# Mixture-of-experts kernel: small remainder tiles two to a tile in the last round but one, five token blocks needed before the first tiles, three blocks placed without pauses

## What is computed

```python
x = x + jnp.tanh(g_xattn[0]) * _L0_xattn_ref(ctx_512, _layernorm(x, axis=-1), L0_xattn_W, L0_xattn_b)
x = x + jnp.tanh(g_ffn[0]) * _L0_ffn_ref(_layernorm(x, axis=-1), L0_ffn_w_router, ...)

scores = jax.nn.sigmoid(xf @ w_router)
sfc = scores + corr_bias          # choice: 4 best of 8 groups, then the 6 best experts in them
combine = jnp.zeros((T, E), dtype=x.dtype).at[jnp.arange(T)[:, None], topk_idx].add(topk_w)
g = jnp.einsum('th,ehm->etm', xf, gate_w)
u = jnp.einsum('th,ehm->etm', xf, up_w)
eo = jnp.einsum('etm,emh->eth', jax.nn.silu(g) * u, down_w)
routed = jnp.einsum('te,eth->th', combine, eo)
shared = jax.nn.silu(xf @ sh_gate_w) * (xf @ sh_up_w) @ sh_down_w
```

## Time and profile before

| | |
|---|---|
| median of 3 runs | 258.53 us |
| the profiled execution | 258.77 us |
| its span in the profile | 256.9 us |
| TensorE matmuls busy | 219.3 us (85%) |
| GpSimd busy | 157.4 us (61%) |
| VectorE busy | 129.4 us (50%) |
| ScalarE busy | 80.0 us (31%) |
| mean granted TensorE clock | 0.924 |
| gate and up instructions (line 742) | 224, four for each of 56 tiles |
| moved by DMA | 53.72 MB |

### The profile page before, as it was taken

How to read it: one execution, slowest core, us unless ns; L and a number is a source line. 1 busy time by engine, 2 the same in 40 slices (tenths; PEclk the granted TensorE clock), 3 DMA queues, 4 the chain that set the end, 5 groups by cost and what they waited for, 6 DMA issues and landing times.

```text
span 256.9 us, 5093 instructions
## 1 busy us (share of the span) xinstructions
PE 219.3 (85%) x1043; PEld 170.9 (67%) x1044; DVE 129.4 (50%) x528; ACT 80.0 (31%) x222; POOL 157.4 (61%) x188
## 2 busy tenths in 40 slices
PE   7996987994799789999999999999999998996000
PEld 6895776882677467877777777778777776774000
DVE  2898886929554444434443444434343443343334
ACT  3636121011010124343434344344444433442000
POOL 6352888787878873528468488566575665475300
PEclk9779799997599999999999999999999999999555
DMA  6999999999997649999998768777667675257767
GB/s 200 250 260 278 407 376 331 332 373 292 318 351 255 195 151 337 253 303 214 249 231 158 126 112 154 121 121 119 107 117 108 110 119 81 35 64 153 175 168 260
DMA packets 41018, 53.72 MB, mean 209 GB/s; under 512 B 5134, under 2 KB 35438, under 8 KB 40998
## 3 DMA queue, kind: packets, MB, share of 16 engines
q1 hardware_dynamic: 25520, 30.99, 41.7%
q0 software_dynamic: 11280, 18.36, 35.7%
q10 hardware_dynamic: 4198, 4.15, 5.9%
HBM read 31.72 MB, written 21.77 MB: 208 GB/s over the span
## 4 chain that ended last, share of the span: by engine, by line
PE 61%; DVE 17%; DMA 8%; issue 5%; another core or an unknown queue 4%; POOL 4%; ACT 1%; SPq 0%; ACTq 0%; POOLq 0%; DVEq 0%
PE pG L742 26%; PE pY L756 18%; PE pX L736 5%; DMA sum_dram<-xnT,idx 5%; PE pH L750 5%; PE pG L765 3%; PE pY L692 2%; PE pY L784 2%; DMA wgu<-sum_dram 2%; POOL rows_dram L432 1%; DMA wij<-in_L_xattn_W_dram 1%; PE pH L773 1%; DVE wgu L1013 1%; POOL rstd L418 1%
## 5 line engine op out<-in xcount | busy, mean ns | idle before, releaser
L445 POOL DMA_INDIRECT sum_dram<-xnT,idx x56 | 86.7, 1548 | 57.2 <-ACT xnT L559 30.8
L742 PE MATMUL pG<-wgu,sdown 128*128 x224 | 75.8, 461 | 1.4 <-issue 1.4
L432 POOL DMA_INDIRECT rows_dram<-rows,row_i x48 | 47.5, 989 | 18.3 <-issue 11.3
L756 PE MATMUL pY<-wd,sup 88*128 x224 | 57.5, 379 | 0.0
L1134 DVE COPY sup<-pH 88x256 f32<-88x256 f32 x56 | 23.5, 420 | 59.0 <-PE pH L750 51.3
L742 PEld LDWEIGHTS pG<-wgu,sdown 128*128 128x128 f32 x224 | 38.5, 191 | 13.9 <-issue 2.0
L559 ACT ACTIVATE xnT<-pY,wt 128x256 f32<-128x256 f32 x56 | 26.5, 473 | 54.1 <-issue 22.4
L756 PEld LDWEIGHTS pY<-wd,sup 88*128 88x128 f32 x224 | 38.0, 190 | 3.2 <-issue 0.2
L750 PEld LDWEIGHTS pH<-ident,sgate 128*88 128x88 f32 x112 | 18.0, 161 | 13.6 <-DVE sgate L1130 0.5
L552 ACT ACTIVATE sgate<-pG 128x176 f32<-128x176 f32 x56 | 17.8, 317 | 27.1 <-PE pG L742 26.0
L547 ACT ACTIVATE sdown<-pX 128x256 f32<-128x256 f32 x56 | 21.0, 377 | 4.9 <-PE pX L736 4.5
(11 more groups left out here) (183 smaller groups left out, 246.2 us busy)
## 6 DMA issues: line engine op xcount, KB each, us to landing
wgu<-in_L_ffn_gate_w_dram SPq DMA_DIRECT2D x8, 704.0 KB, 10.0
wgu<-in_L_ffn_up_w_dram SPq DMA_DIRECT2D x8, 704.0 KB, 13.0
wd<-in_L_ffn_down_w_dram SPq DMA_DIRECT2D x8, 640.0 KB
sum_dram<-zeros POOLq DMA_DIRECT2D x3, 1152.0 KB
wgu<-sum_dram SPq DMA_DIRECT2D x12, 256.0 KB, 3.9
xg<-rows_dram SPq DMA_DIRECT2D x16, 144.5 KB
rows<-rows_dram ACTq DMA_DIRECT2D x16, 144.5 KB
rows_dram<-zeros SPq DMA_DIRECT2D x8, 289.0 KB, 4.5
```

What stands on the lines that cost most here:

```text
L432: pool.indirect_dma_start(rows_dram[:, :], bass.IndirectOffsetOnAxis(ap=row_i[:, j, k:k + 1], axis=0), lines[:, j * ROW:j * ROW + LINE], N ...
L445: pool.indirect_dma_start(sums_dram[into[s]][:, :], bass.IndirectOffsetOnAxis(ap=idx[:, s:s + 1], axis=0), y[s], None, compute_op=ALU.add) ...
L742: ins = nc.tensor.matmul(pG[par][:, 0:2 * M].rearrange("t (g m) -> t g m", g=2), xT[:, par, k, :], wgu[:, bass.ds(e, 1), :, k, :].rearrang ...
L756: ins = nc.tensor.matmul(pY[par][:, 0:H], hT[0:MI, par, i, :], wd[:, bass.ds(e, 1), i, :], start=(i == 0), stop=(i == I - 1))
```

## The change

**Shared tiles.** The plan has four segments. A remainder of more than 64 rows is still a tile of its own; remainders of up to 64 rows (SIDE = 64) go two to a tile, into the 8 tiles of the round before the last, which has 16 such sides (entries 112 to 127 of the plan's table). Sides beyond 16 would become whole tiles. In such a turn SyncE loads the two halves of the tile apart (`load_sides`), TensorE does gate and up and down for each half in its own half of the array's columns (`gate_up_sides`, `down_sides`, `tile_position=(0, SIDE)`), ScalarE scales the halves apart (`scale_y_sides`), VectorE picks apart (`take_sides`), and GpSimd makes two adds of 64 rows (`add_side`). The first half's expert has its weights in SBUF at an index read from the table; the second half's weights are loaded again from DRAM into a ring of three (gate and up) and a ring of two (down) buffers (`own_gate_up`, `own_down`). The last round holds whole tiles (`load_final`, `take_final`, `add_final`).

**Blocks.** The tiles that may start early are now those for which the first FIRST = 5 blocks suffice, and the first loads wait for five blocks' scatters. The three blocks after them are scattered without the pause.

The core of the diff:

```diff
-    LEAST = -(-(PAIRS - T) // (P * ROUND)) - 1
+    SIDE = P // 2
+    SHARED = P - 2 * ROUND
+    LEAST = HELD + 1
-    REST = 16 * (J - JH) * TOPK
+    FIRST = JH + 1
+    REST = 16 * (J - FIRST) * TOPK
-    SEGS = 3
+    SEGS = 4
     INTO = [s % SUMS for s in range(ROUND)]
-    INTO_LAST = [2, 0, 1, 2, 0, 1, 0, 1]
+    INTO_SIDES = [(q + 2) % SUMS for q in range(2 * ROUND)]
+    INTO_LAST = [0, 2, 1, 2, 0, 1, 0, 1]
...
             last = load_last(sp)
+            for s in range(3):
+                own_gate_up(s)
+            for s in range(2):
+                own_down(s)
             with sp.Fori(HELD, ROUNDS) as i:
-                with sp.If(i < last + 1):
+                with sp.If(i < last - 1):
                     for s in range(ROUND):
                         load(sp, i * ROUND + s, s, all_placed=True)
+            for s in range(ROUND):
+                load_sides((last - 1) * ROUND + s, s)
+            for n in range(-2, ROUND - 1):
+                if n + 2 < ROUND:
+                    load_final(n + 2)
+                if 3 <= n + 4 < ROUND:
+                    own_gate_up(n + 4)
+                if 2 <= n + 1:
+                    own_down(n + 1)
...
+            def own_gate_up(s):
+                e = own_expert(s)
+                if s >= 3:
+                    sp.wait_ge(s_gu, (last - 1) * ROUND + s - 2)
...
+            def own_down(s):
+                e = own_expert(s)
+                if s >= 2:
+                    sp.wait_ge(s_y, (last - 1) * ROUND + s - 1)
...
             def place(j, k):
-                done = s_scat if j < JH else s_rest
+                done = s_scat if j < FIRST else s_rest
...
-                chain(pool.memset(wj_wide[:, :], 0.0))
+                if j < FIRST:
+                    chain(pool.memset(wj_wide[:, :], 0.0))
...
+            for q in range(2 * ROUND):
+                add_side((last - 1) * ROUND + q // 2, q)
             for s in range(ROUND):
-                add(last * ROUND + s, s, last, INTO_LAST)
+                add_final(last * ROUND + s, s)
...
+            def scale_y_sides(t, s):
+                act.wait_ge(s_y, t + 1)
+                act.wait_ge(s_taken, t + 1)
+                for side in range(2):
+                    q, ps = 2 * s + side, slice(side * SIDE, (side + 1) * SIDE)
+                    act.wait_ge(s_add[q % YRING], (last - 1) * 16 + 16 * (q // YRING))
+                    ins = nc.scalar.activation(y[q % YRING][0:SIDE, :], pY[s % 2][ps, 0:H], ACT.Copy, scale=wt[ps, s:s + 1])
...
+            def gate_up_sides(t, s, e):
+                par = s % 2
+                pe.wait_ge(s_xTc, t + 1)
+                pe.wait_ge(s_owngu[s % 3], 32 * (s // 3 + 1))
+                for k in range(K):
+                    nc.tensor.matmul(pG[par][0:SIDE, 0:2 * M].rearrange("t (g m) -> t g m", g=2), xT[:, par, k, 0:SIDE],
+                                     wgu[:, bass.ds(e, 1), :, k, :].rearrange("p e g m -> p (e g) m"),
+                                     start=(k == 0), stop=(k == K - 1))
+                    ins = nc.tensor.matmul(pG[par][SIDE:P, 0:2 * M].rearrange("t (g m) -> t g m", g=2), xT[:, par, k, SIDE:P],
+                                           own_gu[s % 3][:, :, k, :], start=(k == 0), stop=(k == K - 1),
+                                           tile_position=(0, SIDE))
+                ins.then_inc(s_gu, 1)
...
-            last = load_last(pe)
             with pe.Fori(2, ROUNDS - 1) as i:
-                with pe.If(i < last):
+                with pe.If(i < last - 2):
                     iteration(i)
-            e_last = iteration(last, tiles=ROUND)
+            _, e_side = iteration(last - 2, shared=1)
+            e_side, e_final = iteration(last - 1, shared=2, e_next=e_side)
+            e_last, _ = iteration(last, shared=3, e=e_side, e_next=e_final)
```

On VectorE the plan's segment arithmetic is done for four segments instead of three, with some ten small operations more (`whole`, `small_at`, a fourth row each of `cnt_i`, `past`, `cur`, `picked`, then `shift` and `reach`), and five small operations (`side_of`) stand ahead of the first `choose_groups`. Of these the diff shows:

```diff
+            V.scalar_tensor_tensor(whole[:, :], tend[:, 3, E - 1:E], -2.0 * ROUND, tend[:, 2, E - 1:E],
+                                   op0=ALU.add, op1=ALU.max)
+            V.tensor_scalar(small_at[:, 0:1], part_f[:, :], tend[:, 2, E - 1:E], side_of[:, 3:4], ALU.is_ge, ALU.mult)
+            link(V.tensor_scalar(small_at[:, 1:2], tend[:, 2, E - 1:E], -float(P), side_of[:, 0:1], ALU.add, ALU.mult))
+            link(V.tensor_tensor(small_at[:, 2:3], small_at[:, 0:1], small_at[:, 1:2], ALU.add))
```

More of the change, by code:

```diff
@@ L574, in _, with turn @@
             silu(0, 0)
-            def turn(i, s, left=ROUND, old=2, fetch=()):
+            def turn(i, s, left=ROUND, old=2, fetch=(), shared=0):
                 t = i * ROUND + s
@@ L597, in _ @@
             for s in range(ROUND):
-                turn(last, s, ROUND - s)
-            scale_y(last * ROUND + (ROUND - 1), ROUND - 1, True, last)
+                turn(last - 1, s, left=2 * ROUND, shared=1)
+            for s in range(ROUND):
+                turn(last, s, ROUND - s, shared=2)
+            scale_y(last * ROUND + (ROUND - 1), ROUND - 1, True, last + 1)
         @block.tensor
@@ L1172, in _, with turn @@
             gate(0, 0)
-            def turn(i, s, left=ROUND, first=False):
+            def turn(i, s, left=ROUND, first=False, shared=0):
                 t = i * ROUND + s
@@ L1188, in _ @@
             for s in range(ROUND):
-                turn(last, s, ROUND - s)
+                turn(last - 2, s, shared=1)
+            for s in range(ROUND):
+                turn(last - 1, s, shared=2)
+            for s in range(ROUND):
+                turn(last, s, ROUND - s, shared=3)
             for b in range(B):
```

247 lines of the change are left out of this document (181 added, 66 removed).

## The result

The changed kernel takes **291.6 us** in the median of 4 runs (290.5 to 296.2); the kernel before took 259.2 beside it. The ratio is 1.124, with a 95% interval of 1.115 to 1.132: slower by an eighth, where 251.2 us was forecast. Ratios and intervals in this document leave out executions over 1.5% longer than the fastest of the same kernel beside them, so a ratio need not be the quotient of two medians.

The account below looks back on a forecast made before the run. It took TensorE to bound the main loop. Turns removed -19.96, shared turns +9.4, adds 0, plan +1.8 and seams +1.5 gave -7.3 us, from 258.77 to 251.5, as a median 251.2 us; range 243.5 to 260.5.

Parts of the forecast that it names:

- How many turns go: Main loop: 56 turns become 48, removing eight turns of 2.495 us each, -19.96 us.
- What a shared turn costs: Shared round on TensorE: a shared turn takes 3.67 us instead of 2.495, so eight add +9.4 us.
- The four changes of mode: Shared turn: TensorE runs empty at each change between whole-array transposes and half-array matmuls, 0.66 us per turn.
- The order A1 A2 B1 B2: Shared turn: instructions of the two halves overlap only partly, five slots instead of eight, adding 0.51 us per turn.
- Loops that set a floor: Shared round: down-weight reload, 2.7 us per turn, and SyncE's list, some 3.5 us, stay hidden under the 3.67 us turn.
- Five blocks, no pauses: Start of the tiles: a fifth block costs 0 (up to +1.5 us); dropping pauses frees only GpSimd, 0 (-1 to +1).
- Seams: Loop exits: six absent rounds jumped over instead of three, with stalls at two places, +1.5 us (0 to 3).
- The plan: Routing plan on VectorE, which TensorE waits for: added and wider operations cost +1.8 us (0.8 to 2.8).
- The adds: Shared round's 16 adds of 64 rows just keep up with TensorE; the tail stays at 6.0 us, 0 added.
- that rival: Adds as the bound: with 6.9 us per 64-row add the tail grows by 8.5 us, about 258.5 us; chance 0.11.
- The free overlap: Rival: half-array matmuls run side by side at no price, shared turn 3.0 us, 247.3 us or 244; chance 0.20.
- the slower ones: Rivals: adds as the bound, 258.5 us (0.11); halves in series, 262.5 us (0.14); no fewer rounds, 271 us (0.03).

Follow-up runs that it names:

- e4: Changed kernel loading the second half's weights only for the first three (gate and up) and two (down) sides, then reusing them: 244.4 us, 0.955 of the kernel before.
- f4: f3 with the loops over rounds of all five engines bounded to the rounds this data has: 249.6 us, 0.971 of the kernel before.
- e2: Changed kernel with SyncE issuing the second half's weights ahead of the last round's row tile load: 253.8 us, 0.990 of the kernel before.
- e11: Changed kernel with ScalarE issuing own down weights, SyncE own gate weights ahead of last-round row tiles, and a pause behind every scatter: 248.4 us, 0.975 of the kernel before.
- f1: Kernel before with only the pauses behind the last three blocks' scatters left out, on a chip where tiles start late: 273.7 us, 1.058 of the kernel before.
- f2: Kernel before with five blocks placed ahead of the first tiles, every pause kept, on a chip where tiles start late: 259.2 us, 1.006 of the kernel before.
- e10: Kernel before with five blocks placed ahead of the first tiles, every pause kept, on a chip where nothing starts late: 255.1 us, 0.996 of the kernel before.
- f3: The same kernel as e11, run on a chip where tiles start late: 254.7 us, 0.986 of the kernel before.
- e12: e11 with only TensorE's loop over rounds bounded to the one round this data has: 248.2 us, 0.970 of the kernel before.
- relieved kernels: Changed kernel with ScalarE issuing own down weights, SyncE own gate weights ahead of last-round row tiles; with pauses 0.975 and 0.986 of the kernel before.

## Why the prediction was wrong

- **How many turns go: right.** 160 and 64 gate instructions, 48 turns. The 19.96 us are real: e4's eight shared turns take 25.5 us where 16 whole ones took 39.9, which is the 19.96 less what shared turns cost more. e4 as a whole is at 0.955, f4, which loads every weight, at 0.971.
- **What a shared turn costs: right in its drain, wrong in its overlap, and it didn't matter.** The four changes of mode were put at 0.66 us and measured 0.68. The order A1 A2 B1 B2 was put at 0.51 us per turn and measured 0: halves start 0.01 us apart. So the term is 5.5 us (e4) instead of 9.4.
- **Loops that set a floor: the step that failed.** The working had the down weights' loop at 5.4 us for two turns and SyncE's list at 3.5 us for a turn, both "under the turn", and said that what stands behind a late own_down is only the load of a row tile, so that a slip costs nothing. It looked at what is queued behind the weights and not at what is queued ahead of them. There stood a load that waits for a take of the running turn. The shared turn became 47.8 / 8 = 6.0 us instead of 3.67, which is 47.8 - 19.96 = +27.8 us against a forecast of +9.4, and 6.5 us more in the last round, whose first turns still use own down weights. The prediction's own sign of being wrong, TensorE waiting there for the second half's weights, is what the page shows (20 us). SyncE's list was also too cheap: e2 shows 5.0 to 5.6 us from one row tile's load to the next in a full turn, the first of them without a wait, not 3.5. The run that shows the cause is e2: the order alone takes the shared round from 47.6 to 37.0 us and, with the seven turns behind it, 15.8 us away. e4 and e11 show that the transfers themselves would be in time.
- **Five blocks, no pauses: the second step that failed.** Put at 0, with -1 to +1 for the pauses. On the first chip it was +12.7 us to the first gate, the plan's share included; on chip C f1 shows 14.8 us in the median (273.7 against 258.9) for the pauses alone. The sentence "It frees only GpSimd" assumed that scatters issued faster hurt nobody. On chips B and D that held. On which kind of chip the kernel would run could not be known from the rows; that it landed on one of the slow kind is bad luck on top of the error. The five blocks themselves were rightly put near 0 (f2: 1.006, e10: 0.996).
- **Seams: the mechanism was right, the size was off.** Put at +1.5 us over the kernel before. TensorE's join measures 10.2 - 5.0 = 5.2 us, half of it not the stall but the slower instructions behind it, which the working left out. All whole tiles together (t0 to t32) take 4.6 us more; the kernel before has its own 1.1 us of exit further on, so the term comes to some 3.5 us, by this subtraction. Taking every engine's join away saves 6.6 us in the trace (f3 to f4) and 5.1 in the median, but taking TensorE's alone away only 0.5 in the trace (e11 to e12).
- **The plan: right.** The shared expert's last down group starts at 67.48 instead of 65.90 us, +1.6 where +1.8 was forecast.
- **The adds: right here, for another reason.** A 64-row add takes 1.43 us of GpSimd instead of 1.55, hardly less, so two per turn take nearly the shared turn. In the changed kernel TensorE is so late that they nearly keep up (the last add starts 7.1 us behind the last scaling instead of 6.0). In the relieved kernels they are the next bound, as that rival said, though not evenly: 3.6 us more in f3's tail, 1.0 in f4's.
- **The rivals.** The free overlap was the case of the matmuls, but its price took the weight loop as the floor, 3.0 us. None of the rivals had a queue that waits on itself; the slower ones ended at 258.5, 262.5 and 271.

## What to carry to other kernels

When loads are added to an in-order queue, write down for every added DMA what stands *ahead* of it, and whether one of those waits for something that this DMA feeds. A prefetch that may wait belongs behind every load that the running turn needs; here swapping three calls was worth some 16 us. And a pace between scatters, or a run of skipped loop rounds, looks like idle time, but its price may show on some chips only, or only at the join: measure such an edit alone and on more than one chip.

## What the runs showed of the hardware that was not expected

- Two half-array float32 matmuls with 64 rows each, on different columns, run fully side by side though both use all rows: a pair every 0.30 us, weights loaded for both meanwhile (e4).
- With the last eighteen scatters back to back (1.27 us apart instead of 1.475) one and the same kernel starts its tiles at 84.9 us on chips B and D and at 109.9 on chip C. Kernels with pauses start at 87.1 to 88.5 on B and D and at 93.0 to 100.0 on C. In the hole even SyncE's register instructions start some 0.7 us apart (f1).
- Stepping over six absent rounds leaves TensorE without a matmul for 2.5 us (changed kernel), and the gate group behind takes 2.49 instead of 1.35 us. With that gone, VectorE's own loop end holds TensorE up by 1.7 us (e12). The other engines' share wasn't measured apart.
- An accumulating scatter of 64 rows occupies GpSimd for 1.43 us, one of 128 rows for 1.55: in these two sizes the price goes by the instruction, not the row.
